# A CIN tower on one core: the last third layer of slot a in two halves, around the last second layer of slot b

## The reference

```python
e = jnp.stack([tbl_0[ids[:, 0]], ..., tbl_31[ids[:, 31]]], axis=1)     # x0: 1024 x 32 x 16
for W in (W0, W1, W2):
    xk = jax.nn.relu(jnp.einsum('bmd,bhd,mhk->bkd', x0, xk, W))
    outs.append(jnp.sum(xk, axis=2))
h = jnp.concatenate([jnp.concatenate(outs, axis=1), dense_ctx], axis=1)
h = jnp.maximum(h @ W_top1 + b_top1, 0.0)
h = jnp.maximum(h @ W_top2 + b_top2, 0.0)
y = h @ W_top3
```

## Time and profile before

| | |
|---|---|
| median of 3 runs | 672.56 us (670.64 to 673.87) |
| the profiled execution, its own time | 672.92 us |
| its span | 670.8 us |
| busy PE, DVE, POOL, ACT | 87%, 84%, 70%, 34% of the span |
| mean granted clock of PE | 0.982 |

### The profile page before, as it was taken

How to read it: one execution, slowest core, us unless ns; L and a number is a source line. 1 busy time by engine, 2 the same in 40 slices (tenths; PEclk the granted TensorE clock), 3 DMA queues, 4 the chain that set the end, 5 groups by cost and what they waited for, 6 DMA issues and landing times.

```text
span 670.8 us, 7232 instructions
## 1 busy us (share of the span) xinstructions
PE 581.4 (87%) x2752; PEld 201.3 (30%) x2752; DVE 563.8 (84%) x292; ACT 230.8 (34%) x425; POOL 469.5 (70%) x354
## 2 busy tenths in 40 slices
PE   0037998999989999999999998999989997999967
PEld 0012222233322342233322242233323342233314
DVE  0028998999899997999799997999889996999763
ACT  0103606144261616143161616244261614335031
POOL 6746487868869686878868686878869685836220
PEclk9986999999999999999999999999989999999979
DMA  5498719494685929394684929395684919476000
GB/s 158 123 397 312 279 23 374 179 356 184 226 329 168 385 62 381 135 366 174 234 322 147 399 59 380 145 344 197 227 330 149 400 33 367 165 290 260 1 0 0
DMA packets 54243, 151.94 MB, mean 227 GB/s; under 512 B 9697, under 2 KB 18913, under 8 KB 54210
## 3 DMA queue, kind: packets, MB, share of 16 engines
q1 hardware_dynamic: 46018, 149.39, 59.3%
q0 software_dynamic: 8192, 2.11, 2.8%
HBM read 147.26 MB, written 4.20 MB: 226 GB/s over the span
## 4 chain that ended last, share of the span: by engine, by line
PE 30%; DVE 21%; issue 19%; ACT 8%; POOL 7%; DMA 7%; another core or an unknown queue 3%; SPq 3%; DVEq 0%; POOLq 0%
PE acc L466 27%; DVE zd L357 20%; POOL emb L282 5%; ACT xk_ps L386 4%; POOL zg L294 3%; SPq L246 2%; DMA base<-x_scratch 2%; ACT xk_sb L386 2%; DMA rolled<-x_scratch 2%; DVE zpart L337 1%; DMA x_scratch<-emb 1%; PE mlp L509 1%; DMA emb<-tables_in,index 1%; ACT xk_ps L372 1%
## 5 line engine op out<-in xcount | busy, mean ns | idle before, releaser
L357 DVE TENSOR_TENSOR zd<-rolled,xk_ps 128x2048 f32<-128x2048 f32 x241 | 538.1, 2283 | 91.9 <-ACT xk_ps L386 33.5
L466 PE MATMUL acc<-zd,w_sb 128*64 128x512 f32 x1672 | 400.8, 609 | 44.7 <-ACT relu_ab L393 34.1
L294 POOL TENSOR_TENSOR zg<-rolled,xk_sb 128x1024 f32<-128x1024 f32 x94 | 223.7, 2383 | 111.5 <-ACT xk_sb L386 103.5
L282 POOL DMA_INDIRECT emb<-tables_in,index x256 | 245.6, 959 | 67.9 <-issue 61.9
L466 PEld LDWEIGHTS acc<-zd,w_sb 128*64 128x64 f32 x1672 | 112.7, 138 | 306.8 <-issue 195.7
L386 ACT ACTIVATE xk_ps<-acc 64x512 f32<-64x512 f32 x128 | 73.2, 572 | 106.6 <-PE acc L466 68.0
L466 PE MATMUL acc<-zg,w_sb 128*64 128x512 f32 x376 | 96.7, 592 | 0.7 <-POOL zg L294 0.7
L466 PE MATMUL acc<-zd,w 128*64 128x512 f32 x256 | 62.9, 607 | 38.7 <-issue 37.3
L386 ACT ACTIVATE xk_sb<-acc 64x512 f32<-64x512 f32 x128 | 75.9, 593 | 3.1
L393 ACT ACTIVATE relu_ab<-acc 128x512 f32<-128x512 f32 x48 | 28.7, 598 | 117.5 <-PE acc L466 116.8
L372 ACT COPY xk_ps<-base 128x512 f32<-128x512 f32 x32 | 17.8, 588 | 136.8 <-DMA base<-x_scratch 136.8
(11 more groups left out here) (46 smaller groups left out, 57.3 us busy)
## 6 DMA issues: line engine op xcount, KB each, us to landing
rolled<-x_scratch SPq DMA_DIRECT2D x256, 512.0 KB, 11.1
base<-x_scratch SPq DMA_DIRECT2D x16, 512.0 KB
emb<-tables_in,index POOLq DMA_INDIRECT x256
x_scratch<-emb SPq DMA_DIRECT2D x32, 128.0 KB
w_sb<-w_in SPq DMA_DIRECT2D x2, 512.0 KB
wt<-wtop_in SPq DMA_DIRECT2D x1, 512.0 KB
wt1a<-wtop_in SPq DMA_DIRECT2D x1, 256.0 KB
w<-w0a_in SPq DMA_DIRECT2D x1, 160.0 KB
```

Source lines behind the costliest of these rows:

```text
L282: pool.indirect_dma_start(emb[:, i % 2, c * DIM:(c + 1) * DIM], None, tables, bass.IndirectOffsetOnAxis(index[:, g:g + 1].bitcast(U32), 0) ...
L294: nc.gpsimd.tensor_tensor(zg[:, n % ZG_BUFS, :], rolled[:, s, j, :], xk_sb[:, s, :], ALU.mult).then_inc(zg_ready, 1)
L357: nc.vector.tensor_tensor(zd[:, n % ZD_BUFS, 0:w, :], rolled[:, s, j:j + w, :], repeated(xk_ps[:, s, :], w), ALU.mult).then_inc(zd_ready, 1)
L466: end = nc.tensor.matmul(acc[h * MAPS:(h + 1) * MAPS, s, :], weights, z[:, h * HALF:(h + 1) * HALF], start=(i == 0 and c == 0), stop=(i == ...
```

## The change

(14,2) is cut at chunk 8 into two phases. The first (chunks 0 to 7, all as four DVE items, no POOL chunk) stays where (14,2) was, ahead of (15,1). The second (chunks 8 to 15, three DVE items and two POOL chunks) stands behind (15,1) and ahead of (15,2). Both go into the same accumulation group of slot a's bank: the first sets start and not stop, the second stop and not start. The first is not evacuated, summed or counted; `ended(q)` counts the finished phases for the semaphores `relu_ready` and `reduced`.

```diff
-ORDER += [(STREAMS - 1, 2)]
+ORDER += [(STREAMS - 2, 2), (STREAMS - 1, 2)]
+PARTS = {len(ORDER) - 4: (0, NCH // 2), len(ORDER) - 2: (NCH // 2, NCH)}
+UNFINISHED = [len(ORDER) - 4]
...
-        for stream, layer in ORDER:
-            n = L0CH if layer == 0 else NCH
-            split = n - (POOL_CHUNKS if stream > 1 else POOL_CHUNKS_FIRST)[stream % 2, layer]
-            dve = [("dve", nd + i, j, min(2, split - j)) for i, j in enumerate(range(0, split, 2))]
+        for q, (stream, layer) in enumerate(ORDER):
+            j0, n = PARTS.get(q, (0, L0CH if layer == 0 else NCH))
+            split = n
+            if q not in UNFINISHED:
+                split -= (POOL_CHUNKS if stream > 1 else POOL_CHUNKS_FIRST)[stream % 2, layer]
+            dve = [("dve", nd + i, j, min(2, split - j)) for i, j in enumerate(range(j0, split, 2))]
...
+def ended(q):
+    return sum(x not in UNFINISHED for x in range(q + 1))
...
-                dve.wait_ge(relu_ready, q + 1)
+                dve.wait_ge(relu_ready, ended(q))
...
-                    act.wait_ge(reduced, before + 1)
+                    act.wait_ge(reduced, ended(before))
...
-                evacuate(q)
+                if q not in UNFINISHED:
+                    evacuate(q)
...
-                    pe.wait_ge(relu_ready, before + 1)
+                    pe.wait_ge(relu_ready, ended(before))
...
-                                                   start=(i == 0 and c == 0),
-                                                   stop=(i == len(merged) - 1 and c == w - 1))
+                                                   start=(j + c == 0),
+                                                   stop=(i == len(merged) - 1 and c == w - 1
+                                                         and q not in UNFINISHED))
...
+            phase(len(ORDER) - 2)
             phase(len(ORDER) - 1, late=last_sums)
```

More of the change, by code:

```diff
@@ L103, in sums_at @@
     items = [(q, x) for q in range(len(ORDER)) for x in range(len(PLAN.dve[q]))]
-    at = []
+    at = {}
     for q, (_, layer) in enumerate(ORDER):
+        if q in UNFINISHED:
+            continue
         i = items.index((q, len(PLAN.dve[q]) - 1)) + SUMS_AFTER[layer]
-        at.append(items[i] if i < len(items) else None)
+        at[q] = items[i] if i < len(items) else None
     return at
@@ L358, in _ @@
                                             repeated(xk_ps[:, s, :], w), ALU.mult).then_inc(zd_ready, 1)
-                    for r in range(q):
+                    for r in sums:
                         if sums[r] == (q, x):
                             reduce_d(r)
-            for r in range(len(ORDER)):
+            for r in sums:
                 if sums[r] is None:
@@ L487, in zsum @@
             def zsum(m):
-                pe.wait_ge(reduced, phase_of(2 * m + 1, 2) + 1)
+                pe.wait_ge(reduced, ended(phase_of(2 * m + 1, 2)))
                 if m > 0:
@@ L522, in last_sums @@
             def last_sums():
-                pe.wait_ge(reduced, phase_of(STREAMS - 1, 1) + 1)
+                pe.wait_ge(reduced, ended(phase_of(STREAMS - 1, 1)))
                 half_sums(TILES - 1, stage[0:MAPS, 0:TB], 0)
@@ L542, in _ @@
             pe.wait_ge(last_z01_sb, 1)
-            pe.wait_ge(relu_ready, len(ORDER) - 1)
+            pe.wait_ge(relu_ready, ended(len(ORDER) - 2))
             for c in range(H1 // P):
@@ L546, in _ @@
             pe.wait_ge(y_ready, m)
-            pe.wait_ge(reduced, len(ORDER))
+            pe.wait_ge(reduced, ended(len(ORDER) - 1))
             half_sums(m, mlp[0:MAPS, TB:2 * TB], 2).then_inc(last_z2_done, 1)
```

## The result

The changed kernel takes 661.66 us (median of 6 runs, 660.12 to 663.34) where the kernel before, measured with it, takes 672.2 us (6 runs, 670.64 to 674.21): ratio 0.984, 95% interval 0.981 to 0.987. The forecast was 663.4 in 661.4 to 667.0.

A forecast was written before the change was run, and what follows sets the result against it. Bound: the uncovered evacuation of (15,1), PE idle 5.55 us and then at a fallen clock. Walking the engines gave -9.2 us: 672.92 to 663.7, less 0.36 for the median, 663.4 us; range 661.4 to 667.0.

The forecast's parts named there:

- Both covers: Behind (15,1), 6.9 us of PE work over 5.5 of evacuation; behind (15,0), 3.4 us to spare on PE.
- The sum, -9.2: Last relu, that of (15,2), starts at 653.1 against 662.27; the last MLP behind it stays, 8.5 us.
- The stretch: Time from PE's first matmul of the last (14,2) to the start of the relu of (15,2); predicted 47.1 us.
- The second count: PE's losses at the end added up: 5.5 us idle, 3.0 for six low-clock chunks, about 0.7 of waits in (14,2).
- The first count: Walk through the engines from (14,2) to (15,2): PE through at 652.6, DVE's items at 650.7, engines level; -9.2 us.
- The price of the low clock: PE in (15,2) behind the hole: 1.36 us a chunk, 0.50 more than at full clock.
- rival 4: Added bank alternation keeps PE at 1.2 GHz from (14,2)'s second half through (15,2), 24 chunks: +2.8 us, 675.4; chance 0.03.
- Rival 1: The clock falls once all the same, 6 chunks still run at 1.36 us: -6.2 us, 666.4; chance 0.07.
- Rival 2: DVE becomes the bound of (15,2), two delays of about 1 us each: -7.2 us, 665.4; chance 0.12.
- Rival 3: Filling the hole ahead of (15,2) does nothing, PE being hidden behind DVE: within 0.5%, 672.5 us; chance 0.03.
- The 0.4 us for handovers in (15,2): Allowance for waits between PE and DVE in (15,2), taken from PE's idle times in (14,2): 0.4 us.
- POOL's products of (15,1): The four products still start near 614.5, when chunk 12 has landed, and end at 623.9, so PE doesn't wait.

The follow-up runs named there:

- the move of the whole: Against the kernel before, (14,2) moved uncut behind (15,1), ahead of (15,2); 663.07 us, ratio 1.000 (0.999 to 1.002).
- the second profile of the kernel before: The kernel before run once more without an edit; 662.31 us (10 runs), ratio 0.998, from the start of (14,2) to the last relu 55.9 us.
- the first measurement: Changed kernel 661.66 us beside the kernel before at 672.2; measured again without an edit, 655.66 beside 663.15.
- the two cuts at 12: Changed kernel with (14,2) cut at chunk 12, 660.06 us; the same with two more POOL chunks and one DVE item less in (15,2), 660.96 us.
- The added matmuls: Kernel before with 12 unneeded matmuls between (15,1) and (15,2): all in one half, 666.19 us; in turns on two halves, 661.52 us.

## Why the prediction was right

Step by step, in us from the start of (14,2), predicted and measured in the changed kernel:

| step | predicted | measured |
|---|---|---|
| `mlp1` done | 7.4 | 7.5 (610.05) |
| `mlp2` done | 12.8 | 13.0 (615.61) |
| end of (15,1) on PE | 25.7 | 26.0 (628.58) |
| end of (14,2) on PE | 32.6 | 32.9 (635.44) |
| relu of (15,1) done, PE may go on | 31.2 | 31.4 (633.41 + 0.60) |
| start of the relu of (15,2) | 47.1 | 47.3 |

- The bound was read rightly: an evacuation that nothing covers, and a clock that falls in it. Both covers held: behind (15,1) with 1.4 us to spare, as predicted, behind (15,0) without a wait. The cuts at 12 and 4 and the move of the whole show where each gives way.
- The sum, -9.2, measured -9.0 (56.3 to 47.3), and -8.6 against the second profile of the kernel before. By the medians it is 10.5 us in the first measurement (1.6%, interval 1.3 to 1.9) and 7.5 in the second (1.2%, 1.0 to 1.5 of 663.15, so 6.6 to 9.7); 9.0 us lies in both. The stretch came out 0.2 us longer than predicted, so the 1.7 us by which 661.66 is under 663.4 lie ahead of it, in the part that scatters; the change has no step there.
- The second count, 5.5 for PE's idle time, 3.0 for the clock and 0.7 for waits, came to the right sum by the wrong parts. It put PE's losses in a row as if nothing stood beside them. Measured, the clock is 1.5 to 2.2 and the hole with the waits 6.8: at full clock DVE, which starts 2.4 us behind the evacuation and has 15.4 + 0.6 to 1.2 us to do, is later than PE, and so part of PE's slow chunks was hidden behind it. The first count, which walked both engines and found them level, had this right.
- The price of the low clock, 1.36 us a chunk, was misread. It is the mean over six chunks, the last of which ran after the clock had come back at 651.0. Six chunks at 0.86 are 5.15 us; half of the 6.0 us at the low clock is 3.0, and together they are the 8.15. So a chunk wholly at the low clock takes twice 0.86, 1.72 us. The forecast doesn't hang on the price of one chunk, as it needed only the sum of 3.0, but rival 4 does: 24 such chunks would cost 20.6 us and not 12.0, and 11 of them, not 18, would eat up the gain.
- Rival 1 (the clock falls all the same) and 4 (it stays low) did not come: 1.00 from 602 to 650. What the Trainium skill ("TensorE: Matmul & The Clock Gate", section "A second HAM failure mode: psum-queue depth-cycling") tells of a clock that falls again and again, no run here shows: with the added alternation it stayed at 1.00. Rival 2 came in part: in the last 21.25 us DVE is the later engine up to its fifth item of (15,2), for which PE waits 0.16 us (643.28), and from there on PE works without a wait. The two engines are so level that it costs only some tenths. Rival 3 is refuted by the result: the time fell by 1.6% and not by under 0.5%.
- The 0.4 us for handovers in (15,2) came out at 0.3: from the end of (14,2) on PE to the last relu it is 47.3 - 32.9 = 14.4 us, where 13.7 and twice 0.2 make 14.1. They were worked out from "6 items and chunks" of (14,2), which are five items and two chunks; the 12 chunks they stand for are right.
- POOL's products of (15,1) start when chunk 12 has landed, and no DVE item of (15,1) waits for `rolled`, as predicted.

What stays open is why the part ahead of the stretch varies by up to 10 us between profiles. Two pieces of it can be seen. In the first profile of the kernel before ACT evacuates (0,0) at 49 us, after a wait whose releaser the profile doesn't know; in the second it does so at 44. The two rows:

```profile
49.06 2.36 ACT L386 ACTIVATE xk_ps<-acc 64x512 f32<-64x512 f32 x4 [16.28 <-remote]
```

```profile
43.93 2.35 ACT L386 ACTIVATE xk_ps<-acc 64x512 f32<-64x512 f32 x4 [11.56 <-PE acc L466]
```

The first profile of the changed kernel has the late start too (48.99); the other nine profiles don't (42.7 to 45.1). PE's clock goes with it: over 40 to 60 us its mean is 0.67 and 0.74 in those two profiles and 0.83 to 0.91 in the other ten. Both are of the first measurement, in which the two kernels take 9 and 6 us more than in the second. What holds ACT up there, and whether chip or chance decides it, was not tried.

## What to carry to other kernels

Where two streams alternate to cover each other's turnaround, look at the last turn: the stream that ends last has nobody to cover it, and the price is the turnaround, here 5.5 us on PE and 8.5 on DVE, plus a fallen clock. Work that only has to be done by the end can be cut so that each turnaround gets just its cover; moving it whole only moves the hole. To price such a hole, walk every engine of the pair to the end and take the later one; adding one engine's losses counts what the other hides.

## What the runs showed of the hardware

- Matmuls of 64 output columns into the two halves of the partitions go at twice the pace. The added matmuls took (10.03 - 0.59) / 22 = 0.43 us a record when all wrote partitions 0 to 63, and (5.32 - 0.59) / 23 = 0.21 us when they took turns, which is also the pace of the kernel's own chunks (0.86 us for four records).
- The clock fell to 0.50 in all holes of 5.5 and 6.55 us, and stayed at 1.00 over two of 2.10 us (the two cuts at 12) and over the gap of 2.74 us in the earlier trace rows. It came back 2.8 us after PE had started again in the move of the whole, 4.5 in the second profile of the kernel before and 6.0 in the first. PE lost half of that each time, 1.4, 2.2 and 3.0 us, so what one hole costs varies by 0.75 us between runs of one program.
